# One power and one shift for both norms of a transformer block, with the second norm applied a step sooner

## The chip, the cores and the metric

One core of a Trainium2 chip (trn2). The metric is the device time of one execution in microseconds (us). The engines are TensorE (PE; its weight loads are listed as PEld), VectorE (DVE), ScalarE (ACT), GpSimd (POOL) and SyncE (SP, which here only issues DMAs). Each engine works through its own queue in order; they meet through semaphores.

## The reference

The input x has 4096 tokens of 256 channels. The output is two layers, each with its residual and a layer norm behind it:

```python
x = layernorm(x + attention(x))      # 16 heads of 16, 4 groups of keys and values, a window of 128 tokens
x = layernorm(x + channel_mix(x))    # mean and variance over the 256 channels, eps 1e-5
def channel_mix(x):                  # x_prev is x of the token before
    xr = mu_r * x + (1 - mu_r) * x_prev
    xk = mu_k * x + (1 - mu_k) * x_prev
    return sigmoid(xr @ W_r.T) * (relu(xk @ W_k.T) ** 2 @ W_v.T)
```

The layer norm is (x - m) / sqrt(v + eps), without weights. Softmax runs over the keys of the window.

## The kernel before, in words

The tokens are cut into 32 blocks of 128 (t = 0 to 31); four blocks are a superblock (s, with j = t % 4 as the place in it). The queries, keys and values of a whole superblock are projected at once and some superblocks ahead; so steps with different j carry different extra work. Everything else goes block by block in a software pipeline: `run` (L249) calls `step` of each engine for every t and, behind the last block, for five more steps that only empty the pipeline (L266). Step t holds, each for another block:

- block t + 1: the maxima of its scores (16 tiles in 6 groups: TensorE `max_scores` into PSUM banks, VectorE `tile_max`, L704, and `turn_max`, L711 to L718, whose rows SP brings to the query operand). The first groups wait for `tiles_ahead` (L696), a copy of block t + 2's queries made a step before.
- block t: its 8 score products (L969), the 8 exponentials on ScalarE (`exps`, L535) and the 8 masks on GpSimd (`mask`, L410). Two PSUM banks take turns, so score product i waits for exponential i - 2.
- block t - 1: the product with the values (L983), the copy att_t (ScalarE, L567), its turn back (TensorE, L1040), the division by the sum (VectorE `normalise`, L808 and L814), the turn of the attention (L1048) and its copy (ScalarE, L572).
- block t - 2: the output product (L1081), the first residual y1 (VectorE, L830) with its moments (L723 to L728), the power and the shift on GpSimd (`rstd`, L417 and L419), and the first norm on ScalarE (L582), a single activation with scale rstd and bias shift = -mean x rstd; then its transposition (L1032) and the copy of that (L592).
- block t - 3: the channel mix: difference to the token before (GpSimd, L470), two mixes on VectorE (L780: `mixed(u, 0)` for the r product, `mixed(u, 1)` for the k product), r product (L1059), tanh (ScalarE, L598), k product (L1070), relu and square (ScalarE).
- block t - 4: the second product (L1024), the gate (VectorE, L789), the second residual y2 (L799) with its moments, and on GpSimd its power and shift.
- block t - 5: the second norm (ScalarE, L617) and the store (SP, L342).

The order within a step is written out by hand for each engine, and the change is about these orders:

- VectorE (L834 to L868): max tiles 0 and 1, gate, max tile 2, first residual and moments, max tile 3, mixed(0), max tiles 4 and 5, `turn_max`, mixed(1), rest parts of the projection, `normalise`, `tiles_ahead`, second residual and moments, copy of vals (j = 1), a second rest part (j = 3).
- GpSimd (L473 to L502): difference, masks 0 and 1, (j = 0: a low part, L402), power and shift of block t - 2, mask 2, (j = 2: `x_plus_bo`, L396), masks 3 to 5, low parts, mask 6, power and shift of block t - 4, mask 7.
- ScalarE (L620 to L662): exponentials 0 and 1, (j = 0: a middle part), second norm of block t - 5, exponential 2, first norm, copy of att_t, (j = 3: high part 0, L517), exponential 3, tanh, (j = 0: high part 2), exponentials 4 and 5, middle parts, relu, square, exponential 6, two copies, (j = 3: high part 1), exponential 7.
- TensorE (L1085 to L1136): max scores 0 and 1, second product, max scores 2, score 0, output product, score 1, max scores 3 and 4, values 0, score 2, max scores 5, values 1, (j = 3: projection chunk 0), score 3, r product, (j = 0: chunk 2; j = 1: the turn of the values, L908), score 4, turn of att_t, score 5, k product, score 6, turn of the attention, turn of x2, (j = 3: chunk 1), score 7.

In the steps with j = 0, 1 or 2 the maxima of the next block use three PSUM banks and max scores 5 waits for max tile 2; in steps with j = 3 there are two, and it waits for max tile 3 (L937). Max scores 2 in step j = 2 goes into the bank that `val_copy` (L686) must have read.

Of the kernel before, what the change touches and what calls it, by code (L numbers as in the profile page):

```python
# [24 lines left out]
ALU = mybir.AluOpType  # L25
# [3 lines left out]
P = 128  # L29
# [25 lines left out]
def attention_channel_mix(nc, x_nat, x_feat, w_first, w_rest, out):  # L55
# [25 lines left out]
    with ExitStack() as ctx:  # L81
# [23 lines left out]
        minus_half = sb("minus_half", [P, 1])  # L105
# [25 lines left out]
        mv1 = sb("mv1", [P, 2])  # L131
        var1 = sb("var1", [P, 1])
        rstd1 = sb("rstd1", [P, 1])
        shift1 = sb("shift1", [P, 1])
# [10 lines left out]
        mv2 = sb("mv2", [P, 2])  # L145
        var2 = sb("var2", [P, 1])
        rstd2 = sb("rstd2", [P, 1])
        shift2 = sb("shift2", [P, 1])
# [50 lines left out]
        s_ln1 = sem("s_ln1")  # L199
        s_rstd1 = sem("s_rstd1")  # L200
        s_shift1 = sem("s_shift1")
# [14 lines left out]
        s_ln2 = sem("s_ln2")  # L216
        s_rstd2 = sem("s_rstd2")
        s_shift2 = sem("s_shift2")
# [30 lines left out]
        def run(eng, start, step, tail=None):  # L249
# [16 lines left out]
            for j in range(SB_BLKS, SB_BLKS + 5):  # L266
                step(NSB - 1, j, 1, project=False, coming=False, maxima=False, scores=False)
# [9 lines left out]
        def _(sp):  # L277
# [80 lines left out]
            def step(s, j, par, project, coming, maxima, scores):  # L358
# [19 lines left out]
                if behind(t, j, scores, 5):  # L378
                    store(t - 5, (j - 5) % 2)
# [10 lines left out]
        def _(pool):  # L390
# [65 lines left out]
            def step(s, j, par, project, coming, maxima, scores):  # L456
# [24 lines left out]
                if f2:  # L481
                    rstd(t - 2, var1, mv1, rstd1, shift1, s_ln1, s_rstd1, s_shift1)
# [16 lines left out]
                if f4:  # L499
                    rstd(t - 4, var2, mv2, rstd2, shift2, s_ln2, s_rstd2, s_shift2)  # L500
# [7 lines left out]
        def _(act):  # L508
# [28 lines left out]
            def start():  # L537
                act.dma_start(first[:, :], w_first).then_inc(s_first, 16)
                act.wait_ge(s_const, 1)
                nc.scalar.activation(warm[:, :], minus_half[:, :], ACT.Exp)  # L540
# [18 lines left out]
            def step(s, j, par, project, coming, maxima, scores):  # L559
                t = s * SB_BLKS + j  # L560
                ahead = project and later(s, 1)
                f1, f2, f3, f5 = (behind(t, j, scores, n) for n in (1, 2, 3, 5))
# [12 lines left out]
                def first_norm(u):  # L575

                    act.wait_ge(s_shift1, u + 1)
# [4 lines left out]
                    nc.scalar.activation(x2[:, u % 3], y1[:, :], ACT.Identity, bias=shift1[:, 0:1],  # L582
# [43 lines left out]
                if f5:  # L626
                    second_norm(t - 5)
# [554 lines left out]
```

## Time and profile before

| what | us |
|---|---|
| median of 3 runs | 453.26 |
| the 3 runs | 449.74, 453.81, 453.26 |
| span of the profiled execution | 449.1 |
| steps with j = 0, 1, 2, 3 of the superblock from 179.6 | 12.3, 11.0, 14.4, 14.0 |
| a step without projection work | 9.9 |

The span is that of the instructions of one execution. No time of its own is given for the profiled execution; the run closest to its span took 449.74, that is 0.6 more. A row of the timeline has the start, the duration, the engine and line, and in brackets how long the engine was idle before the instruction and what ended that. "xN" means N instructions merged in one row, whose duration runs from the first one's start to the last one's end. A row of windows has the stretch, its length, each engine's busy time, and the granted clock of TensorE as a share of 2.4 GHz (PEclk).

### The profile page before, as it was taken

To read this page: it belongs to the slowest core of one execution; us is meant where nothing else is said; L and a number is where in the kernel's file an instruction comes from. 1 tells how busy PE (TensorE), PEld (TensorE's weight loads), DVE (VectorE), ACT (ScalarE), POOL (GpSimd) and SP (SyncE) were. 2 spreads that over 40 slices of the span, in tenths; PEclk is the share of its full clock that TensorE was granted. 3 is DMA by queue.
4 is the path that set the end of the run, shared out by engine and by line. 5 is a ranking of instruction groups with operands and counts; after the bars stand their busy time and mean duration, and the time that the engine had idled before them with its cause. 6 is when DMAs were issued, how large, how long until landed. Compare 5 with 4: busy or idle time off the path is not lost.

```text
span 449.1 us, 8432 instructions
## 1 busy us (share of the span) xinstructions
PE 407.7 (91%) x2542; PEld 251.9 (56%) x2542; DVE 344.6 (77%) x852; ACT 272.8 (61%) x566; POOL 291.2 (65%) x466
## 2 busy tenths in 40 slices
PE   8976999997999979997999979997999979999853
PEld 3444546664556656564556665564656656665532
DVE  5765775898678976899688986799878988996551
ACT  2512567775667747764677657666577657778522
POOL 4552666776487856677487766688487767876531
PEclk9986899998999989999999989999999989999995
DMA  8484585412733175321753146421823144000000
GB/s 324 115 141 91 134 148 138 100 49 46 140 101 84 50 94 146 82 66 43 110 163 86 49 74 152 87 60 47 120 65 94 49 62 70 14 13 27 12 23 23
DMA packets 50892, 39.25 MB, mean 87 GB/s; under 512 B 33696, under 2 KB 42400, under 8 KB 50720
## 3 DMA queue, kind: packets, MB, share of 16 engines
q1 hardware_dynamic: 50416, 37.93, 38.9%
q10 hardware_dynamic: 432, 0.79, 0.6%
q8 instruction: 20, 0.33, 0.3%
q14 instruction: 24, 0.20, 0.2%
HBM read 26.38 MB, written 12.06 MB: 86 GB/s over the span
## 4 chain that ended last, share of the span: by engine, by line
PE 64%; DVE 19%; ACT 6%; issue 6%; DMA 2%; POOL 1%; SPq 1%; ACTq 0%; DVEq 0%; POOLq 0%
PE av_ps L983 11%; PE score_ps L969 9%; PE proj_ps L893 8%; PE max_ps L952 6%; PE gen L1070 6%; PE gen L1024 6%; PE gen L1081 5%; PE gen L1059 4%; DVE neg_max L704 4%; DVE q_tiles L696 3%; DVE max_parts L711 3%; PE max_ps L943 3%; ACT parts L517 2%; DVE mix L780 2%; PE av_ps L1040 2%
## 5 line engine op out<-in xcount | busy, mean ns | idle before, releaser
L410 POOL TENSOR_SCALAR_AFFINE_SELECT probs<-probs 128x512 f32<-128x512 f32 x252 | 168.2, 678 | 108.0 <-ACT probs L535 105.7
L535 ACT ACTIVATE probs<-score_ps 128x512 f32<-128x512 f32 x252 | 148.4, 598 | 86.0 <-PE score_ps L969 85.6
L969 PE MATMUL score_ps<-qs,ks 98*128 98x512 bf16 x252 | 99.8, 398 | 2.2 <-ACT probs L535 1.4
L704 DVE TENSOR_REDUCE neg_max<-max_ps 128x3 f32<-128x480 f32 x144 | 87.4, 631 | 12.3 <-PE max_ps L952 12.1
L983 PE MATMUL av_ps<-probs,vals 128*32 128x512 f32 x504 | 67.0, 605 | 0.9 <-POOL probs L410 0.8
L969 PEld LDWEIGHTS score_ps<-qs,ks 98*128 98x128 bf16 x252 | 25.0, 100 | 57.3 <-ACT probs L535 47.9
L1070 PE MATMUL gen<-mix,rest_w 128*128 128x128 f32 x256 | 38.7, 299 | 16.9 <-DVE mix L780 15.5
L952 PE MATMUL max_ps<-ks,q_tiles 96*128 96x160 bf16 x416 | 52.3, 243 | 0.0
L417 POOL TENSOR_TENSOR rstd<-var,minus_half 128x1 f32<-128x1 f32 x64 | 35.7, 558 | 21.7 <-DVE var L728 20.8
L1070 PEld LDWEIGHTS gen<-mix,rest_w 128*128 128x128 f32 x256 | 35.4, 208 | 22.7 <-DVE mix L780 17.8
L780 DVE SCALAR_TENSOR_TENSOR mix<-diff,first,x_t 128x128 f32<-128x128 f32 x128 | 43.8, 385 | 0.0
L952 PEld LDWEIGHTS max_ps<-ks,q_tiles 96*128 96x128 bf16 x416 | 37.9, 103 | 8.2 <-issue 1.9
L677 DVE SCALAR_TENSOR_TENSOR rest<-proj_ps,first,parts 128x512 f32<-128x512 f32 x19 | 14.3, 751 | 35.5 <-ACT parts L517 32.4
L893 PE MATMUL proj_ps<-x_t,first 128*128 128x512 f32 x76 | 38.3, 628 | 0.7 <-DMA first<-w_first 0.7
L943 PE MATMUL max_ps<-edge_mask,ident_b 128*128 128x192 bf16 x138 | 35.2, 255 | 3.2 <-issue 2.1
L1024 PE MATMUL gen<-rest_w,act_k 128*128 128x256 f32 x128 | 35.9, 405 | 2.1 <-ACT act_k L609 2.0
L402 POOL TENSOR_TENSOR parts<-rest,parts 128x512 bf16<-128x512 f32 x24 | 30.7, 1282 | 10.5 <-ACT parts L528 10.5
L1059 PE MATMUL gen<-rest_w,mix 128*128 128x256 f32 x128 | 34.3, 390 | 3.0 <-DVE mix L780 3.0
L1081 PE MATMUL gen<-rest_w,att_c 128*128 128x256 f32 x128 | 32.9, 379 | 0.0
L696 DVE COPY q_tiles<-qs 96x2048 bf16<-96x2048 bf16 x32 | 27.3, 853 | 5.0 <-DMA qs<-q_parts 5.0
L603 ACT ACTIVATE relu_k<-gen 128x256 f32<-128x256 f32 x32 | 12.7, 397 | 29.8 <-PE gen L1070 29.8
L582 ACT ACTIVATE x<-y,shift,rstd 128x256 f32<-128x256 f32 x32 | 19.2, 599 | 17.4 <-POOL shift L419 16.6
(86 smaller groups left out, 663.2 us busy)
## 6 DMA issues: line engine op xcount, KB each, us to landing
qs<-q_parts SPq DMA_DIRECT2D x48, 192.0 KB, 6.1
q_parts<-parts SPq DMA_DIRECT2D x48, 128.0 KB, 2.2
x_t<-x_feat SPq DMA_DIRECT2D x8, 512.0 KB, 3.7
x_in<-x_nat SPq DMA_DIRECT2D x8, 512.0 KB, 4.5
out<-out_t SPq DMA_DIRECT2D x32, 128.0 KB, 2.0
ks<-k_parts SPq DMA_DIRECT2D x42, 80.0 KB, 2.9
qs<-q_parts SPq DMA_DIRECT2D x42, 64.0 KB, 2.2
k_parts<-parts SPq DMA_DIRECT2D x8, 192.0 KB, 2.8
```

The lines of the kernel that those rows point to most:

```text
L410: nc.gpsimd.affine_select(out=v, in_=v, compare_op=ALU.is_ge if i % 2 else ALU.is_gt, fill=0.0, base=0, pattern=[[0, HPG], [sign, BLK]], c ...
L535: nc.scalar.activation(probs[:, buf, i], score_ps[i % 2][:, :], ACT.Exp, scale=SCALE).then_inc(s_exp, 1)
L704: nc.vector.tensor_reduce(neg_max[:, TPB * i:TPB * i + n], max_bank(t, j, i)[:, 0:n * TILE_KEYS].rearrange("p (n k) -> p n k", k=TILE_KEYS ...
L780: nc.vector.scalar_tensor_tensor(out=mix[:, w, c], in0=diff[:, c], scalar=small_cols[:, MU_COL + w * DC + c:MU_COL + w * DC + c + 1], in1= ...
L893: ins = nc.tensor.matmul((ps or proj_ps)[:, 0:SB], wqkv[:, c, m * P:(m + 1) * P], x_t[:, par, c], start=(c == 0), stop=(c == DC - 1))
L952: ins = nc.tensor.matmul(dst, q_tiles[:, j % 2, tile], ks[0:ROWS, par, g, k0:k0 + TILE_KEYS], start=False, stop=(k == len(tiles) - 1), ski ...
L969: nc.tensor.matmul(score_ps[i % 2][:, :].rearrange("p (h q) -> p h q", q=BLK), ks[0:ROWS + MPARTS, par, g, k0:k0 + BLK], qs[0:ROWS + MPART ...
L983: ins = nc.tensor.matmul(av_ps[g * VCOL:(g + 1) * VCOL, :], vals[:, pk, jk, g, :], probs[:, j % 2, 2 * g + half], start=(half == 0 or not ...
L1024: ins = nc.tensor.matmul(gen0[:, 0:D], act_k[:, c], w_t[:, 2, c], start=(c == 0), stop=(c == DC - 1))
L1059: ins = nc.tensor.matmul(gen0[:, 0:D], mix[:, 0, c], w_t[:, 0, c], start=(c == 0), stop=(c == DC - 1))
L1070: ins = nc.tensor.matmul(gen0[:, o * BLK:(o + 1) * BLK], w_t[:, 1, c, o * P:(o + 1) * P], mix[:, 1, c], start=(c == 0), stop=(c == DC - 1))
L1081: ins = nc.tensor.matmul(gen1[:, 0:D], att_c[:, c], wo[:, c], start=(c == 0), stop=(c == DC - 1))
```

## The change

The variables of both norms get a second column (column 0 is the first norm's, column 1 the second's). VectorE computes the second residual and its moments directly behind the first one's, no longer at the end of the step. GpSimd waits for both variances and takes one power over both columns, where the first power was; its own shifts go. VectorE computes both shifts in one instruction between max tiles 4 and 5. ScalarE applies the second norm, now of block t - 4, between the tanh and the high part or exponential 4, and SP stores it in that step. One step fewer empties the pipeline. At either end of the sequence, where only one of the two blocks exists, a single column is used.

```diff
@@ run
-            for j in range(SB_BLKS, SB_BLKS + 5):
+            for j in range(SB_BLKS, SB_BLKS + 4):
@@ SP, step
-                if behind(t, j, scores, 5):
-                    store(t - 5, (j - 5) % 2)
+                if behind(t, j, scores, 4):
+                    store(t - 4, (j - 4) % 2)
@@ GpSimd
-            def rstd(u, var, mv, out_, shift, ready, done, shifted):
-
-                pool.wait_ge(ready, u * 3 + 3)
-                nc.gpsimd.tensor_tensor(out_[:, :], var[:, :], minus_half[:, :], ALU.pow).then_inc(done, 1)
-                pool.wait_ge(done, u + 1)
-                nc.gpsimd.tensor_scalar(shift[:, :], mv[:, 0:1], out_[:, 0:1], -1.0, ALU.mult,
-                                        ALU.mult).then_inc(shifted, 1)
+            def roots(t, a, b):
+
+                for i, u in enumerate((t - 2, t - 4)):
+                    if a <= i < b:
+                        pool.wait_ge(s_var[i], u + 1)
+                nc.gpsimd.tensor_tensor(rstd[:, a:b], var[:, a:b], minus_half[:, a:b], ALU.pow).then_inc(s_rstd, 1)
...
-                if f2:
-                    rstd(t - 2, var1, mv1, rstd1, shift1, s_ln1, s_rstd1, s_shift1)
+                if f2 or f4:
+                    roots(t, 0 if f2 else 1, 2 if f4 else 1)
                 if scores and t:
                     mask(t, 2, j % 2)
...
                     mask(t, 6, j % 2)
-                if f4:
-                    rstd(t - 4, var2, mv2, rstd2, shift2, s_ln2, s_rstd2, s_shift2)
                 if scores:
                     mask(t, 7, j % 2)
@@ ScalarE
                 def second_norm(u):
 
-                    act.wait_ge(s_shift2, u + 1)
+                    act.wait_ge(s_shift, u + 3)
...
-                if f5:
-                    second_norm(t - 5)
                 if scores and t:
                     exps(t, 2, j % 2)
                 if f2:
                     first_norm(t - 2)
...
                 if f3:
                     tanh(t - 3)
+                if f4:
+                    second_norm(t - 4)
                 if ahead and j == 0:
                     high_part(s + 1, 2)
@@ VectorE
+            def shifts(t, a, b):
+
+                dve.wait_ge(s_rstd, t - 1)
+                nc.vector.scalar_tensor_tensor(out=shift[:, a:b], in0=mv[:, a:b, 0], scalar=-1.0, in1=rstd[:, a:b],
+                                               op0=ALU.mult, op1=ALU.mult).then_inc(s_shift, 1)
...
                 if f2:
                     first_residual(t - 2)
+                if f4:
+                    second_residual(t - 4)
                 if maxima:
                     tile_max(t + 1, jn, 3)
                 if f3:
                     mixed(t - 3, 0)
                 if maxima:
                     tile_max(t + 1, jn, 4)
+                if f2 or f4:
+                    shifts(t, 0 if f2 else 1, 2 if f4 else 1)
+                if maxima:
                     tile_max(t + 1, jn, 5)
                     turn_max(t + 1, j + 1)
...
                     tiles_ahead()
-                if f4:
-                    second_residual(t - 4)
                 if ahead and j == 1:
                     val_copy(s + 1, 1 - par)
```

## Rows read from the trace of the kernel before

**Rows 1.** The page, busy time of each engine (share of span, instructions).

```profile
span 449.1 us, 8432 instructions
...
PE 407.7 (91%) x2542; PEld 251.9 (56%) x2542; DVE 344.6 (77%) x852; ACT 272.8 (61%) x566; POOL 291.2 (65%) x466
```

**Rows 2.** Windows by step: j = 0, 1, 2, 3, and plain step 29.

```profile
179.60:191.90 12.30, 12.00 (x80) 7.38 (x79) 10.17 (x26) 8.99 (x20) 8.30 (x13) 1.00 0.38 81
191.90:202.90 11.00, 10.77 (x80) 7.18 (x79) 10.17 (x28) 7.56 (x17) 8.71 (x16) 1.00 0.27 70
202.90:217.30 14.40, 11.82 (x76) 7.98 (x75) 12.34 (x28) 7.62 (x17) 9.89 (x15) 0.88 0.40 72
217.30:231.30 14.00, 13.89 (x84) 8.06 (x83) 9.72 (x27) 9.73 (x21) 9.15 (x15) 1.00 0.59 137
...
390.50:400.40 9.90, 9.90 (x76) 6.76 (x75) 9.06 (x26) 7.61 (x17) 7.71 (x14) 1.00 0.06 17
```

**Rows 3.** Timeline of plain step 29: start us, duration us, engine, line.

```profile
390.23 1.03 PE L1081 MATMUL gen<-rest_w,att_c 128*128 128x256 f32 x4
...
391.60 0.42 DVE L830 TENSOR_TENSOR y<-gen,x_bo 128x256 f32<-128x256 f32 x1
...
392.79 0.15 DVE L728 TENSOR_SCALAR var<-mv 128x1 f32<-128x1 f32 x1
...
393.95 0.65 DVE L704 TENSOR_REDUCE neg_max<-max_ps 128x3 f32<-128x480 f32 x1
394.12 0.60 ACT L582 ACTIVATE x<-y,shift,rstd 128x256 f32<-128x256 f32 x1
...
395.70 0.38 ACT L598 ACTIVATE tanh_r<-gen 128x256 f32<-128x256 f32 x1
...
396.38 1.05 PE L1070 MATMUL gen<-mix,rest_w 128*128 128x128 f32 x8
...
397.80 0.84 DVE L799 SCALAR_TENSOR_TENSOR y<-gated,x 128x256 f32<-128x256 f32 x1
```

**Rows 4.** The page, costliest groups: the powers on GpSimd.

```profile
L417 POOL TENSOR_TENSOR rstd<-var,minus_half 128x1 f32<-128x1 f32 x64 | 35.7, 558 | 21.7 <-DVE var L728 20.8
```

**Rows 5.** Timeline of step 12 (j = 0).

```profile
181.92 1.16 POOL L402 TENSOR_TENSOR parts<-rest,parts 128x512 bf16<-128x512 f32 x1
...
186.50 0.69 ACT L517 ACTIVATE parts<-proj_ps,first 128x512 bf16<-128x512 f32 x1 [0.63 <-PE proj_ps L893]
...
188.65 0.44 PE L1048 MATMUL av_ps<-ident,att 128*128 128x128 f32 x2 [0.20 <-DVE att L814]
...
189.50 1.37 DVE L799 SCALAR_TENSOR_TENSOR y<-gated,x 128x256 f32<-128x256 f32 x1
```

**Rows 6.** Waits, whole trace: waiter, releaser, us in total, times, longest.

```profile
PEld proj_ps L943 <- DVE vals L686: 3.2, 6, 0.5
```

**Rows 7.** Timeline of step 14 (j = 2), and the k product of step 22.

```profile
207.13 2.36 POOL L396 TENSOR_TENSOR x_bo<-x_in,rest_w 128x1024 f32<-128x1024 f32 x1
207.24 2.28 DVE L711 CAST max_parts<-neg_max 128x16 bf16<-128x16 f32 x1
...
211.50 2.03 PE L1070 MATMUL gen<-mix,rest_w 128*128 128x128 f32 x8 [2.58 <-DVE mix L780]
...
314.71 1.16 PE L1070 MATMUL gen<-mix,rest_w 128*128 128x128 f32 x8 [2.57 <-DVE mix L780]
```

**Rows 8.** Windows: TensorE behind the hole of step 14, and the emptying pipeline.

```profile
211.50:214.90 3.40, 3.40 (x14) 2.94 (x15) 2.23 (x7) 1.30 (x4) 0.00 (x0) 0.51 0.68 124
...
430.00:436.00 6.00, 3.61 (x18) 2.50 (x18) 2.37 (x10) 2.43 (x6) 2.44 (x5) 1.00 0.03 9
```

**Rows 9.** Timeline of step 15 (j = 3): max scores 5.

```profile
220.07 0.10 PEld L943 LDWEIGHTS max_ps<-edge_mask,ident_b 128*128 128x128 bf16 x1 [0.19 <-DVE neg_max L704]
```

**Rows 10.** Timeline of the emptying pipeline, steps 33 and 34.

```profile
430.17 1.13 PE L1059 MATMUL gen<-rest_w,mix 128*128 128x256 f32 x4 [2.00 <-DVE mix L780]
...
436.76 0.42 DVE L799 SCALAR_TENSOR_TENSOR y<-gated,x 128x256 f32<-128x256 f32 x1
```

More of the change, by code:

```diff
@@ L104, in attention_channel_mix @@
         w_t = rest_w[:, D + DC * D:].rearrange("p (w c n) -> p w c n", w=3, c=DC)
-        minus_half = sb("minus_half", [P, 1])
+        minus_half = sb("minus_half", [P, 2])
         warm = sb("warm", [P, 1])
@@ L130, in attention_channel_mix @@
         stats1 = sb("stats1", [P, 6])
[L131 to L134, printed above, removed]
+        mv = sb("mv", [P, 2, 2])
+        var = sb("var", [P, 2])
+        rstd = sb("rstd", [P, 2])
+        shift = sb("shift", [P, 2])
         x2 = sb("x2", [P, 3, D])
@@ L198, in attention_channel_mix @@
         s_y1 = sem("s_y1")
-        s_ln1 = sem("s_ln1")
-        s_rstd1 = sem("s_rstd1")
-        s_shift1 = sem("s_shift1")
+        s_ln = [sem("s_ln1"), sem("s_ln2")]
+        s_var = [sem("s_var1"), sem("s_var2")]
+        s_rstd = sem("s_rstd")
+        s_shift = sem("s_shift")
         s_x2 = sem("s_x2")
@@ L539, in start @@
                 act.wait_ge(s_const, 1)
-                nc.scalar.activation(warm[:, :], minus_half[:, :], ACT.Exp)
+                nc.scalar.activation(warm[:, :], minus_half[:, 0:1], ACT.Exp)
                 act.wait_ge(s_first, 16)
@@ L561, in step @@
                 ahead = project and later(s, 1)
-                f1, f2, f3, f5 = (behind(t, j, scores, n) for n in (1, 2, 3, 5))
+                f1, f2, f3, f4 = (behind(t, j, scores, n) for n in (1, 2, 3, 4))
                 def att_t_copy():
@@ L575, in first_norm @@
                 def first_norm(u):
-                    act.wait_ge(s_shift1, u + 1)
+                    act.wait_ge(s_shift, u + 1)
                     if u >= 3:
@@ L581, in first_norm @@
                         act.wait_ge(s_y2, u - 2)
-                    nc.scalar.activation(x2[:, u % 3], y1[:, :], ACT.Identity, bias=shift1[:, 0:1],
-                                         scale=rstd1[:, 0:1]).then_inc(s_x2, 1)
+                    nc.scalar.activation(x2[:, u % 3], y1[:, :], ACT.Identity, bias=shift[:, 0:1],
+                                         scale=rstd[:, 0:1]).then_inc(s_x2, 1)
                 def x2_t_copy(u):
@@ L611, in second_norm @@
                 def second_norm(u):
-                    act.wait_ge(s_shift2, u + 1)
+                    act.wait_ge(s_shift, u + 3)
                     if u >= 2:
                         act.wait_ge(s_store[u % 2], 16 * (u // 2) + 1)
-                    nc.scalar.activation(out_t[:, u % 2], y2[:, :], ACT.Identity, bias=shift2[:, 0:1],
-                                         scale=rstd2[:, 0:1]).then_inc(s_out, 1)
+                    nc.scalar.activation(out_t[:, u % 2], y2[:, :], ACT.Identity, bias=shift[:, 1:2],
+                                         scale=rstd[:, 1:2]).then_inc(s_out, 1)
                 if scores and t:
@@ L800, in second_residual @@
                                                    in1=x2[:, u % 3], op0=ALU.mult, op1=ALU.add).then_inc(s_y2, 1)
-                    moments(u, y2, s_y2, stats2, mv2, var2, s_ln2)
+                    moments(1, u, y2, s_y2, stats2)
                 def normalise():
@@ L831, in first_residual @@
                                             ALU.add).then_inc(s_y1, 1)
-                    moments(u, y1, s_y1, stats1, mv1, var1, s_ln1)
+                    moments(0, u, y1, s_y1, stats1)
                 if maxima:
```

19 lines of the change are left out of this document (6 added, 13 removed).

## The prediction

> **What bounds the kernel now.** I read first the page's busy shares: TensorE is at 91% of a 449.1 us span and the next engine, VectorE, at 77% [rows 1]. So the question is in which steps TensorE waits. The steps of one superblock (four blocks), as windows of the trace, give 12.3, 11.0, 14.4 and 14.0 us for j = 0, 1, 2, 3, with TensorE busy 12.00, 10.77, 11.82 and 13.89 us; a plain step without projection work takes 9.9 us and TensorE is busy for all of it [rows 2]. Only j = 2 has a real hole. Everywhere else TensorE's queue is full, but only just, and that is what the change must be held against: which results come to it with how little to spare.
>
> The timeline of a plain step shows that [rows 3]. The chain of the first norm is: output product ends 391.26, first residual y (VectorE) 391.60, its variance ends 392.94, power and shift on GpSimd, norm on ScalarE at 394.12. Behind the norm, in ScalarE's queue, stand the copy of att_t, one exponential and the tanh, which ends at 396.08. TensorE's k product (L1070) waits for that tanh and starts at 396.38. **Slack: 0.30 us**, for everything that makes the norm later. The k product is followed by work of TensorE without a gap up to the next output product.
>
> **The change part by part.**
> *GpSimd.* 64 powers of 0.558 us [rows 4] become 34 (one in each of the steps 2 to 35), and 64 shifts go. Nothing of this is on the path by itself: GpSimd is 65% busy [rows 1] and its last mask of a step has cover. I cost the saving at 0 to 0.3 us a step, and take 0. But the power now waits for both variances, and the masks 2 to 7 stand behind it.
>
> *VectorE, second residual moved forward.* It is now directly behind the first residual's moments, ahead of max tile 3, mixed(0) and max tile 4. Residual to variance takes 1.34 us undisturbed (391.60 to 392.94 [rows 3]; the second residual alone 0.42 in [rows 10]), and 1.8 where the second residual takes 0.84 as in rows 3. So the second variance is 1.35 to 1.8 us later than the first.
>
> *VectorE, shift.* The instruction isn't in the trace of before; nearest are the variance's 0.15 us [rows 3] below, and, held by GpSimd, a cast of 16 columns that took 2.28 [rows 7] above. I take 0.15 where no long GpSimd instruction runs. It stands behind max tile 4. From the variance's end to that tile's end are 1.66 us (392.94 to 394.60 [rows 3]), longer than the power (0.08 + 0.56) that used to be all that lay there, with GpSimd's shift.
>
> *Plain step, sum.* The first residual can start 0.3 sooner (391.31), as VectorE's end of the step is emptier. 391.31 + 1.34 + 1.30 to 1.75 (second residual and moments) + 1.66 + 0.2 (shift) + 0.05 = 395.86 to 396.31 for the norm, against 394.12: 1.74 to 2.2 later. Less the slack of 0.30 the k product is 1.45 to 1.9 late, and all of TensorE with it. The second norm (0.60, the same form as the first), which used to sit in a hole of ScalarE ahead of exponential 2, now stands between tanh and exponential 4: 0 to 0.2. I take **1.65 us** for a plain step, bounds 1.1 and 2.1. Nothing takes it back: what left VectorE's end of the step was beside a full TensorE. Steps 28, 29, 30 and 27: 4 x 1.65 = 6.6. Step 31 (no max tiles) 0.9; steps 2 and 3, where only the shift is late, together 0.4.
>
> *j = 0.* GpSimd's low part runs 181.92 to 183.08, exactly where the second residual now comes; the one that ran beside such an instruction took 1.37 [rows 5]. So its variance ends about 184.3, tile 4 about 186.0, the norm starts about 186.2 (before 184.03), the tanh ends 188.15, and behind it now stand the second norm and only then ScalarE's high part: 188.65 against 186.50 [rows 5]. VectorE's rest part, the softmax division and TensorE's turn of the attention, which waited 0.20 for it [rows 5], follow the high part one to one: up to 2.1 us. If the second residual gets in ahead of the low part, 1.1. I take 1.9. 6 steps: 11.4.
>
> *j = 1.* Here the move also gives something: VectorE entered this step late because the second residual, 1.37 long, ended step 0, and the copy of vals stood behind it in step 1, for which TensorE waited 3.2 us in 6 times [rows 6]. The first residual starts 1.0 sooner, so the norm is late by 0.9 to 1.3 only; k product +0.75, second norm in ScalarE's queue +0.2, vals -0.3: 0.65, bounds 0 and 1.1. 6 steps: 3.9.
>
> *j = 2.* TensorE waits 2.58 us for mixed(1), since the cast L711 took 2.28 beside GpSimd's x_bo of 2.36 [rows 7]. Now power and mask 2 end 0.7 later, so x_bo runs about 207.85 to 210.2, and the shift, due at 208.4, falls into it. I let it be held to the end: norm 210.25, tanh ends 212.2, k product 212.25 against 211.50: +0.7. The rows show a cast with one input held, and the second residual with two (0.84, 1.37). The Trainium skill ("GPSIMD Engine Reference", section Key points) says that GpSimd shares its SBUF interfaces with VectorE and collides with instructions in a two-port mode or with two SBUF inputs; the new shift has two (mv and rstd), so the rule speaks for held. If it were not, the cast behind it would be held and k would come about 0.5 late, 1.2 us less in all. Bounds 0 and 1.3. 6 steps: 4.2.
>
> *j = 3.* With two banks only, max scores 5 waits for max tile 3; before, that wait was 0.19 us as the tile ran straight behind the first variance [rows 9]. Now the second residual is ahead of it: 1.35 late, and behind max scores 5 stand the value products, the projection, the r and k products. The second norm delays ScalarE's relu and high part by another 0 to 0.5. 1.6, bounds 1.3 and 2.0. 5 steps (7 to 23): 8.0.
>
> *The end.* From step 32 on, engines wait for one another in one chain. In step 32 the norm of block 30 is late and the turn of att_t with it: 1.0. In step 33 TensorE waited 2.00 us for mixed(0) [rows 10], and block 29's second residual is now ahead of that mix: 1.05. In step 34 the same with block 30: 1.35. In step 35 power, shift, norm and store of block 31 come one after another as before; that they belong to step 35 and not 36 is worth 0.1. The store's DMA was behind nothing on SP's queue that matters. Sum 3.4, bounds 2.4 and 4.0.
>
> *The clock.* In 5 of the 6 steps with j = 2 the granted clock fell to 0.51 (1.2 instead of 2.4 GHz) behind the 2.58 us hole; 3.40 us of TensorE work then did what 1.7 do at full clock [rows 8]. It is a near thing: behind 2.57 us of waiting the k product of another superblock took 1.16 instead of 2.03 us [rows 7]. After the change the hole is cut in two (about 2.2, then the turn of att_t, then 0.3), so I let 2 of the 5 falls go: -3.4, bounds -8.5 and 0.
>
> **Sum.** 6.6 + 0.9 + 0.4 + 11.4 + 3.9 + 4.2 + 8.0 + 3.4 - 3.4 = +35.4, so a span of 484.5 from 449.1. The runs shown have 449.74, 453.81 and 453.26; which was profiled is not given. The median is 4.2 above the span, and I add the sum to it: 453.3 + 35.4 = **489 us**. All parts at their lower bounds, with all five falls gone: 4.4 + 0.6 + 0 + 6.6 + 0 + 0 + 6.5 + 2.4 - 8.5 = +12; all at the upper: 8.4 + 1.2 + 0.8 + 12.6 + 6.6 + 7.8 + 10 + 4 = +51. They won't all lie on one side; its own range is 478 to 501.
>
> **The rivals.**
> *Half of it is hidden (chance 0.17).* The second residual slips in ahead of the low part, the shift ahead of x_bo, ScalarE finds holes for the second norm, and all clock falls go. For it: VectorE's end of each step is 1.8 us emptier. Against: the first norm's wait is in every step. Near the lower bounds, some +16: 469.
> *The clock falls in more places (0.11).* Every step now has a hole of about 1 us on TensorE. One fall more in each step with j = 0 and j = 3: 11 x 1.7 = 19, so 508. Against: from 430 to 436 TensorE was busy for 3.61 of 6.00 us, with a hole of 2.00, and the clock stayed at 1.00 [rows 8, 10].
> *Not slower (0.05).* The mechanism: what limits the steps is VectorE's tail (second residual, then vals and the first max tiles), and the norm's lateness disappears in ScalarE's queue. Then step 1 gets back 1.05 and vals 0.3, 8 us in six superblocks: 445. It decides from the point where the norm is less than 0.30 us late; the rows make it 1.7.
> *The merge is not worth what it says (inside the first).* GpSimd's saved 0.9 us a step doesn't appear in the time at all; what does is only where the second residual stands.
>
> **How the numbers follow.** Forecast 0.67, the others 0.17, 0.11, 0.05. The range for 8 in 10 runs from the centre of the half-hidden case to short of the clock case: 469 to 504. A measurement of this kernel tells about 1% from no change. Faster by over 1%: 0.04; within 1%: 0.02; slower: 0.94.
>
> **What would show it.** Right: in a plain step the norm (L582) starts 1.7 to 2.2 us later behind the output product, tanh ends just ahead of the k product, step length about 11.5; in j = 3 TensorE waits about 1.4 for max tile 3; ScalarE's largest new wait is for VectorE's shift; a second residual of over 1 us in j = 0; a shift of 1 us or more in j = 2 alone. Wrong: plain steps still at 9.9 us, or a shift that starts right behind the power, or TensorE's share still over 90%.

## The result, and the profile after

The changed kernel takes 497.23 us (median of 4 runs, 495.6 to 503.29); the kernel before, with one more run beside it, 451.8. The ratio is **1.097** (95% interval 1.089 to 1.105): slower, as forecast (489 us, range 469 to 504). Executions of one kernel differ in how often TensorE's clock fell, and the profiled ones of three experiments below (the shift sooner, the second residual behind the first mix, and the shift behind max tile 5 in the steps with j = 0) lie above the medians of their runs, so their step lengths may hold more falls than a median run does. The profiled execution has a span of 495.0 us, 45.9 more than before; the forecast's sum was +35.4.

The page of the kernel after, with its largest waits (waiter, releaser, us in total, times, longest):

```profile
span 495.0 us, 8400 instructions
...
PE 423.2 (85%) x2540; PEld 254.8 (51%) x2542; DVE 340.2 (69%) x886; ACT 268.3 (54%) x566; POOL 259.4 (52%) x372
...
L573 ACT ACTIVATE x<-y,shift,rstd 128x256 f32<-128x256 f32 x32 | 19.2, 599 | 83.3 <-DVE shift L724 83.3
...
L413 POOL TENSOR_TENSOR rstd<-var,minus_half 128x2 f32<-128x2 f32 (+1 forms) x34 | 23.2, 683 | 56.8 <-DVE var L719 56.8
```

```profile
ACT x L573 <- DVE shift L724: 83.3, 31, 5.3
...
PEld gen L1059 <- DVE mix L777: 33.1, 26, 3.7
...
PEld av_ps L1040 <- ACT att_t L558: 26.3, 19, 3.1
```

GpSimd's work fell from 291.2 to 259.4 us and nothing of it came back as time: every engine is busy for a smaller share of the span, since each waits for another. TensorE is down from 91% [rows 1] to 85%. ScalarE waits 83.3 us for the new shift. TensorE waits for two things for which it hardly waited before: its weight loads wait 33.1 us for the mix ahead of the r product (6.2 before) and 26.3 for the copy of att_t behind the norm (2.5 before).

Windows by step, for the same steps as [rows 2] (12 to 15, j = 0 to 3, and the plain step 29):

```profile
190.90:205.10 14.20, 12.34 (x79) 7.29 (x79) 11.47 (x30) 9.02 (x19) 8.76 (x13) 1.00 0.33 69
205.10:216.50 11.40, 10.97 (x80) 7.00 (x79) 9.22 (x28) 7.31 (x16) 5.80 (x9) 1.00 0.27 72
216.50:231.30 14.80, 11.79 (x76) 8.00 (x75) 11.13 (x28) 7.42 (x16) 9.50 (x12) 0.88 0.33 56
231.30:246.80 15.50, 13.99 (x84) 8.07 (x83) 9.52 (x29) 9.72 (x20) 8.01 (x13) 1.00 0.69 136
...
424.90:436.30 11.40, 10.59 (x75) 6.63 (x75) 8.89 (x27) 7.31 (x16) 6.38 (x11) 1.00 0.05 14
```

Step lengths against the forecast (I take each step's start from ScalarE's first exponential in the two timelines and add up the steps of one kind):

| steps | forecast, us | measured, us |
|---|---|---|
| j = 0, six | +11.4 | +11.9 |
| j = 1, six | +3.9 | +3.0 |
| j = 2, six, clock falls included | 4.2 - 3.4 = +0.8 | +7.8 |
| j = 3, five | +8.0 | +7.5 |
| plain 27 to 30 | +6.6 | +6.3 |
| 2 and 3 | +0.4 | 0 |
| 31 and the emptying of the pipeline | +4.3 | +8.1 |
| ahead of step 2 | 0 | +1.4 |

Of the terms of the sum, five hold to within a microsecond. Two failed by more: j = 2 by 7.0 us and the end by 3.8, and TensorE's clock has a part in both. Ahead of step 2, where the changed code does not run, the profiles of all the kernels here lie between 51.1 and 55.0 us, so +1.4 says nothing of the change.

The timeline of the plain step 29, which answers to [rows 3]:

```profile
424.74 1.03 PE L1081 MATMUL gen<-rest_w,att_c 128*128 128x256 f32 x4
...
425.80 0.42 DVE L827 TENSOR_TENSOR y<-gen,x_bo 128x256 f32<-128x256 f32 x1 [0.39 <-PE gen L1081]
...
427.12 0.53 DVE L796 SCALAR_TENSOR_TENSOR y<-gated,x 128x256 f32<-128x256 f32 x1
...
428.44 0.15 DVE L719 TENSOR_SCALAR var<-mv 128x1 f32<-128x1 f32 x1
...
428.74 0.70 POOL L413 TENSOR_TENSOR rstd<-var,minus_half 128x2 f32<-128x2 f32 x1 [1.36 <-DVE var L719]
...
429.73 1.13 PE L1059 MATMUL gen<-rest_w,mix 128*128 128x256 f32 x4 [0.42 <-DVE mix L777]
430.16 0.15 DVE L724 SCALAR_TENSOR_TENSOR shift<-mv,rstd 128x2 f32<-128x2 f32 x1
...
430.35 0.60 ACT L573 ACTIVATE x<-y,shift,rstd 128x256 f32<-128x256 f32 x1 [1.82 <-DVE shift L724]
...
431.47 0.66 PE L1040 MATMUL av_ps<-ident,att_t 128*128 128x128 f32 x4 [0.39 <-ACT att_t L558]
...
431.81 0.38 ACT L589 ACTIVATE tanh_r<-gen 128x256 f32<-128x256 f32 x1
...
432.33 1.13 PE L1070 MATMUL gen<-mix,rest_w 128*128 128x128 f32 x8
```

From the end of the output product (425.77) to the norm are 4.58 us, against 2.86 before (394.12 - 391.26): 1.72 later, the forecast had 1.74 to 2.2. The tanh ends at 432.19 and the k product starts at 432.33, right behind it, 1.44 later than before counted from the output product. Between power's end (429.44) and shift (430.16) lie 0.72 us in which the shift waits for nothing but its turn behind max tile 4. TensorE stands twice, for the mix and for att_t.

The norm's path was not the only tight one. In the kernel before, VectorE's mixed(1), for which the k product waits as well, ended at 396.00, that is 0.38 us ahead of the k product (396.38), hardly more than the 0.30 that the tanh had:

```profile
395.43 0.57 DVE L780 SCALAR_TENSOR_TENSOR mix<-diff,first,x_t 128x128 f32<-128x128 f32 x2
```

In the kernel after, mixed(1) ends at 431.71 and the tanh at 432.19, so the norm's path is the later one, by 0.48.

In step 12 (j = 0) the second residual runs beside GpSimd's low part and takes 1.37, and the high part, now behind the second norm, starts 199.80 - 190.92 = 8.9 us into the step instead of 7.0. In step 15 (j = 3) max scores 5 waits for max tile 3, 1.69 instead of 0.19 [rows 9]:

```profile
193.34 1.16 POOL L396 TENSOR_TENSOR parts<-rest,parts 128x512 bf16<-128x512 f32 x1
193.41 1.37 DVE L796 SCALAR_TENSOR_TENSOR y<-gated,x 128x256 f32<-128x256 f32 x1
...
235.74 0.10 PEld L943 LDWEIGHTS max_ps<-edge_mask,ident_b 128*128 128x128 bf16 x1 [1.69 <-DVE neg_max L695]
```

Step 14 (j = 2), which answers to [rows 7]:

```profile
221.80 2.34 POOL L390 TENSOR_TENSOR x_bo<-x_in,rest_w 128x1024 f32<-128x1024 f32 x1
221.82 2.34 DVE L724 SCALAR_TENSOR_TENSOR shift<-mv,rstd 128x2 f32<-128x2 f32 x1
224.20 0.60 ACT L573 ACTIVATE x<-y,shift,rstd 128x256 f32<-128x256 f32 x1 [4.02 <-DVE shift L724]
...
225.32 1.11 PE L1040 MATMUL av_ps<-ident,att_t 128*128 128x128 f32 x4 [2.58 <-ACT att_t L558]
...
226.66 1.82 PE L1070 MATMUL gen<-mix,rest_w 128*128 128x128 f32 x8
```

A shift over two columns, 0.15 us elsewhere, takes 2.34 beside x_bo: it starts 0.02 behind x_bo and ends 0.02 behind it. It was so in all six steps of this kind (2.33 or 2.34), and so was TensorE's wait for att_t, 2.57 or 2.58.

### The profile page after: what moved, and what is told of

Read it like the earlier page. It is cut to its first block, busy times and chain, and to the rows that moved or that the text cites. A ratio compares the mean times of both kernels' runs of the same rounds, so it can differ in the third digit from the quotient of the medians.

```text
span 495.0 us, 8400 instructions
## 1 busy us (share of the span) xinstructions
PE 423.2 (85%) x2540; PEld 254.8 (51%) x2542; DVE 340.2 (69%) x886; ACT 268.3 (54%) x566; POOL 259.4 (52%) x372
## 4 chain that ended last, share of the span: by engine, by line
PE 40%; DVE 32%; ACT 14%; issue 9%; DMA 2%; POOL 1%; SPq 1%; ACTq 0%; DVEq 0%; POOLq 0%
DVE neg_max L695 7%; DVE stats L714 5%; PE gen L1024 5%; PE gen L1070 5%; PE score_ps L969 5%; PE gen L1081 5%; DVE y L796 4%; ACT probs L526 4%; PE proj_ps L893 3%; PE max_ps L952 3%; DVE shift L724 3%; ACT parts L508 3%; PE av_ps L1040 3%; DVE y L827 3%; DVE mix L777 2%
## 5 line engine op out<-in xcount | busy, mean ns | idle before, releaser
L526 ACT ACTIVATE probs<-score_ps 128x512 f32<-128x512 f32 x252 | 146.8, 599 | 95.3 <-PE score_ps L969 95.3
L573 ACT ACTIVATE x<-y,shift,rstd 128x256 f32<-128x256 f32 x32 | 19.2, 599 | 83.3 <-DVE shift L724 83.3
L1059 PE MATMUL gen<-rest_w,mix 128*128 128x256 f32 x128 | 37.3, 416 | 24.2 <-DVE mix L777 24.2
L413 POOL TENSOR_TENSOR rstd<-var,minus_half 128x2 f32<-128x2 f32 (+1 forms) x34 | 23.2, 683 | 56.8 <-DVE var L719 56.8
L943 PE MATMUL max_ps<-edge_mask,ident_b 128*128 128x192 bf16 x138 | 34.7, 251 | 12.3 <-DVE neg_max L695 8.8
L1070 PE MATMUL gen<-mix,rest_w 128*128 128x128 f32 x256 | 42.1, 317 | 1.1 <-ACT tanh_r L589 1.1
L1070 PEld LDWEIGHTS gen<-mix,rest_w 128*128 128x128 f32 x256 | 38.6, 225 | 7.8 <-issue 7.0
L1059 PEld LDWEIGHTS gen<-rest_w,mix 128*128 128x128 f32 x128 | 23.2, 197 | 36.9 <-DVE mix L777 33.1
L777 DVE SCALAR_TENSOR_TENSOR mix<-diff,first,x_t 128x128 f32<-128x128 f32 x128 | 38.3, 340 | 0.2 <-issue 0.2
L1040 PE MATMUL av_ps<-ident,att_t 128*128 128x128 f32 x128 | 22.1, 299 | 17.9 <-ACT att_t L558 17.9
L396 POOL TENSOR_TENSOR parts<-rest,parts 128x512 bf16<-128x512 f32 x24 | 30.7, 1285 | 10.2 <-ACT parts L519 10.2
```

The source lines that it names most:

```text
L526: nc.scalar.activation(probs[:, buf, i], score_ps[i % 2][:, :], ACT.Exp, scale=SCALE).then_inc(s_exp, 1)
L777: nc.vector.scalar_tensor_tensor(out=mix[:, w, c], in0=diff[:, c], scalar=small_cols[:, MU_COL + w * DC + c:MU_COL + w * DC + c + 1], in1= ...
L1059: ins = nc.tensor.matmul(gen0[:, 0:D], mix[:, 0, c], w_t[:, 0, c], start=(c == 0), stop=(c == DC - 1))
L1070: ins = nc.tensor.matmul(gen0[:, o * BLK:(o + 1) * BLK], w_t[:, 1, c, o * P:(o + 1) * P], mix[:, 1, c], start=(c == 0), stop=(c == DC - 1))
```

## The experiments

The theories. **Theory 1**: what counts is VectorE's order; the second residual and two max tiles stand ahead of the shift, and the second residual ahead of max tile 3 and mixed(0). **Theory 2**: what counts is that GpSimd's power waits for both variances. **Theory 3**: the shift on VectorE and the second norm's place on ScalarE cost as much as the move. All ratios below are to the kernel before, run on the same chip.

### One power or two

```diff
-                if f2 or f4:
-                    roots(t, 0 if f2 else 1, 2 if f4 else 1)
+                if f2:
+                    roots(t, 0, 1)
                 if scores and t:
                     mask(t, 2, j % 2)
+                if f4:
+                    roots(t, 1, 2)
```

> The changed kernel, but GpSimd takes the first norm's power right behind the first variance (one column), and the second's behind mask 2; VectorE's order and the one shift stay. Theory 1 (VectorE's order holds the norm: second residual, max tiles 3 and 4 stand ahead of the shift): the shift starts where it did, so 494 to 500 us, at most 3 us gained by earlier masks. Theory 2 (GpSimd's joint wait for both variances holds it): the first power is 1.4 us sooner in each step, so about 30 us gained, near 467.

486.62 us, ratio 1.069 (1.062 to 1.076), between the two expectations, so neither number came true. The step lengths say where: the plain steps are still 11.5 us, j = 0 still 14.2, j = 3 still 15.5, j = 1 still 11.5. Only j = 2 changed, in its windows beside a plain step:

```profile
214.40:227.70 13.30, 10.62 (x76) 6.67 (x75) 10.79 (x27) 7.30 (x17) 9.44 (x13) 1.00 0.28 54
414.40:425.90 11.50, 10.67 (x76) 6.71 (x75) 8.99 (x27) 7.34 (x17) 6.89 (x12) 1.00 0.05 14
```

```profile
222.74 0.66 PE L1042 MATMUL av_ps<-ident,att_t 128*128 128x128 f32 x4 [2.23 <-ACT att_t L560]
```

So theory 2 falls for the steps of every kind but that one: the power was 1.4 us sooner and the plain step didn't move. In j = 2 the shift is held for 1.99 instead of 2.34 us, and TensorE's wait for att_t is 2.23 or 2.24 instead of 2.58. In four of the six such steps there was no fall of the clock and they took 13.3 us, where the changed kernel, with a fall in each, took 14.8 to 16.3.

### The shift sooner

```diff
                 if f3:
                     mixed(t - 3, 0)
+                if f2 or f4:
+                    shifts(t, 0 if f2 else 1, 2 if f4 else 1)
                 if maxima:
                     tile_max(t + 1, jn, 4)
-                if f2 or f4:
-                    shifts(t, 0 if f2 else 1, 2 if f4 else 1)
-                if maxima:
                     tile_max(t + 1, jn, 5)
```

> The changed kernel with the one shift directly behind mixed(0), ahead of max tile 4. Theory 1: the norm is 0.5 to 0.65 us sooner in each of some 28 steps, and in j = 2 the shift gets in ahead of x_bo, so 12 to 20 us gained: 477 to 485. Theory 2: the power is the limit and it ends just ahead of this place; 0 to 4 us gained: 493 to 497.

Ratio 1.088 (1.076 to 1.100), median 500.74: both numbers are missed, and by the ratio this kernel can't be told from the changed one. The line of the shift in this kernel (minimum, median, maximum in ns):

```profile
L724 DVE SCALAR_TENSOR_TENSOR shift<-mv,rstd x34: 147/587/593, 57.3 to 499.6; 128x2 f32<-128x2 f32 x30, 128x1 f32<-128x1 f32 x4
```

The shift no longer meets x_bo, but now it meets mask 2, which GpSimd starts the moment the power is done, and takes 0.59 instead of 0.15. The norm came only 0.13 us sooner in a plain step (4.42 against 4.55 us behind y1). In j = 2 it came 2.3 us sooner (4.42 against 6.74) and the step still took 15.4: there the cast behind the shift is held instead, and the k product waits 2.40 us for its other operand, mixed(1). And in four of the steps with j = 0 the clock fell, and they took 15.8 to 16.4 instead of 14.2.

### The second residual moved, alone

```diff
                 if f2:
                     first_residual(t - 2)
+                if f4:
+                    second_residual(t - 4)
...
                     tiles_ahead()
-                if f4:
-                    second_residual(t - 4)
```

(in the kernel before, with its own powers and shifts)

> The kernel before, with one edit: VectorE's second residual and moments stand behind the first ones; powers, shifts and second norm as before. Theory 1: mixed(0) is 1.35 to 1.8 us late but the norm isn't; plain steps +0.5 (the tanh behind the r product), j = 3 +1.4 (max tile 3), j = 0 +0.5, pipeline's end +2.4: 15 to 22 us slower than before, 467 to 474. Theory 2: the move costs nothing by itself, 450 to 455.

487.51 us, ratio **1.070** (1.064 to 1.077): the right sign, but 32 us where 15 to 22 were expected. The move alone makes 32 of the 45 us. A plain step:

```profile
417.90:429.00 11.10, 10.47 (x76) 6.73 (x75) 8.96 (x26) 7.70 (x17) 7.71 (x15) 1.00 0.05 15
```

and in its timeline:

```profile
421.40 0.60 ACT L582 ACTIVATE x<-y,shift,rstd 128x256 f32<-128x256 f32 x1
...
422.68 1.13 PE L1059 MATMUL gen<-rest_w,mix 128*128 128x256 f32 x4 [0.44 <-DVE mix L780]
...
423.87 0.60 PE L1040 MATMUL av_ps<-ident,att_t 128*128 128x128 f32 x4
...
424.88 1.16 PE L1070 MATMUL gen<-mix,rest_w 128*128 128x128 f32 x8 [0.19 <-DVE mix L780]
```

Here the norm is on time (2.7 us behind the output product), and yet the step is 1.2 longer: the r product waits for mixed(0), and then the k product for mixed(1), which stands behind everything else on VectorE. So in the plain step **two** paths lead from the moved residual to the k product, by the norm and by the mixes. The mixes' path costs 1.2 alone, and the norm's on top of it brings the step to 11.4; what the norm's would cost alone was not run. My expectation had counted only the r product's lateness.

The same holds for j = 0, and there it changes the account. In step 12 of this kernel, which starts at 188.16 and takes 14.1 us:

```profile
194.09 1.13 PE L1059 MATMUL gen<-rest_w,mix 128*128 128x256 f32 x4 [1.55 <-DVE mix L780]
...
195.06 1.88 PE L893 MATMUL proj_ps<-x_t,first 128*128 128x512 f32 x4
...
196.97 0.69 ACT L517 ACTIVATE parts<-proj_ps,first 128x512 bf16<-128x512 f32 x1 [1.33 <-PE proj_ps L893]
```

The norm is on time (4.66 us into the step, 4.52 before) and the second norm is out of the way, and yet the high part starts 8.8 us into the step, as in the changed kernel (8.9; before 7.0). It waits for projection chunk 2, which stands behind the r product on TensorE, and the r product waits 1.55 us for mixed(0). The move alone makes 10.9 of the 11.9 us of the steps with j = 0, and all of the loss with j = 3 (7.9, the changed kernel 7.5).

### Idle work for TensorE while the pipeline empties

```diff
+                if not scores and j > SB_BLKS:
+                    keep_running(max_ps[0], 4)
```

(behind the r product, the k product and the turn of x2)

> The changed kernel with 4 idle matmuls (512 columns, bf16, 0.22 us each at full clock) behind the r product, the k product and the turn of x2 in steps 33 to 35. If the end's 8 us instead of the 3.4 forecast come from the clock, which fell at 470.6 and stayed at 1.2 GHz, the clock now stays up longer and 3 to 6 us go: 491 to 494. If they come from waits alone, the time is the same or up to 2 us longer.

494.72 us, ratio 1.088 (1.079 to 1.096); the interval overlaps that of the changed kernel, so the total tells little. The windows do. Of the changed kernel, the end:

```profile
470.60:495.00 24.40, 12.82 (x34) 8.57 (x34) 6.27 (x24) 4.80 (x11) 2.50 (x4) 0.50 0.05 16
```

and of this one:

```profile
476.60:492.60 16.00, 10.65 (x53) 6.23 (x51) 4.62 (x16) 3.12 (x8) 1.79 (x3) 1.00 0.05 17
```

The clock came back to 1.00. The clock fell inside the wait for block 30's mixed(0), as in the changed kernel, and was back at 1.00 after 6.8 us. From the first mix of block 31 to its gate are 6.2 us here and 8.4 in the changed kernel. That is 2.2 us for the clock in that stretch. From step 31 to the end only 1.4 are gained, so 0.8 was lost again elsewhere; there the k product of block 30, behind idle matmuls at half clock, started 0.9 later behind the r product than in the changed kernel.

### One power for t - 2 and t - 5

The second norm's power can be shared with the first without moving the residual, if it takes the block whose variance was finished at the end of the step before:

```diff
-                for i, u in enumerate((t - 2, t - 4)):
+                for i, u in enumerate((t - 2, t - 5)):
...
                     tiles_ahead()
+                if f4:
+                    second_residual(t - 4)
```

(and second norm, shift, store and the emptying steps for t - 5 in place of t - 4), once with the shift behind max tile 4 and once directly behind mixed(0).

> One power and one shift as in the changed kernel, but for the first norm of block t-2 and the second of t-5, so VectorE's second residual can stay at the end of the step as before; shift behind max tile 4, second norm behind the tanh. Theory 1 (where the second residual stands makes most of the loss): 3.3 us from y1 to norm instead of 2.5, so 0.2 to 0.5 us a step: 0.5 to 2.5% slower than before. Theory 3 (the shift on VectorE and the second norm in ScalarE's queue cost as much as the move): 4% slower or more.

> As the one with t-5, and the shift directly behind mixed(0). Theory 1: mask 2 on GpSimd holds the shift (0.59 instead of 0.15 as in the run with the early shift), norm 2.9 to 3.1 us behind y1, inside or just beyond the slack of 0.3: within 1% of before. Theory 3: 3% slower or more.

Ratios **1.006** (1.003 to 1.010) and **0.996** (0.992 to 1.000). Both hold for theory 1, and theory 3 falls: with the second residual where it was, one power, one shift on VectorE and the second norm behind the tanh stay within 1% of the time before. With the late shift a plain step took 10.4 us, the norm 3.54 behind y1 (before: 2.52); with the early one 9.9 and 2.54. In single steps they are not free. In the profile of the second version only the clock gains, with two falls in the steps with j = 2 instead of five, while its steps with j = 0 took 13.1 instead of 12.3; the first version had three such falls.

### x_plus_bo in four pieces, before and after

```diff
-                if ahead and j == 2:
-                    x_plus_bo(s + 1, 1 - par)
...
                     mask(t, 6, j % 2)
+                if ahead:
+                    x_plus_bo_piece(s + 1, 1 - par, j)
```

(a piece adds one block of 256 columns and waits for that block's old x_bo to be read; s_xbo counts blocks)

> The kernel before with x_plus_bo (2.36 us in the steps with j = 2) cut into four pieces of one block each (about 0.6 us), one in each step, behind mask 6. If the hole in j = 2 comes from VectorE being held by that one GpSimd instruction, these steps fall from 14.4 (12.8 without a clock fall) to 10 to 10.5 us, no clock falls remain there, and the piece costs 0 to 0.2 a step: 4 to 6% faster than before. If it is the work itself and not its place, no change.

> The changed kernel with the same four pieces. The shift is nowhere over 1 us, the steps with j = 2 become like the plain ones, 11.4 to 11.8 us instead of 14.8 to 16.3, no clock falls there: 20 to 25 us less than the changed kernel, so 4 to 5.5% slower than before. If j = 2 is long for another reason (the second residual's place), under 8 us less.

Before with the pieces: 430.27 us, ratio **0.943** (0.937 to 0.950). After with the pieces: 474.05, ratio 1.042 (1.035 to 1.048). The steps with j = 2 in the first:

```profile
193.40:203.90 10.50, 10.10 (x76) 6.70 (x75) 9.65 (x28) 7.58 (x17) 8.39 (x15) 1.00 0.41 75
```

10.5 instead of 14.4 [rows 2], in all six of them, and no fall of the clock between 46.4 and 408.2 us. In the second they took 11.4 in all six, as long as a plain step. So the one GpSimd instruction of 2.36 us, where it stood, had cost each kernel about 25 us. The edit makes it shorter and moves it at once; which of the two counts was not tried apart. The change's own loss, with this out of the way, is about 10% (1.042 / 0.943), much as with it.

### The second residual behind the first mix

```diff
-                if f4:
-                    second_residual(t - 4)
                 if maxima:
                     tile_max(t + 1, jn, 3)
                 if f3:
                     mixed(t - 3, 0)
+                if f4:
+                    second_residual(t - 4)
```

> The changed kernel with VectorE's second residual and moments behind max tile 3 and mixed(0) instead of ahead of them; shift still behind max tile 4, so the norm is as late as in the changed kernel (4.5 us behind y1), while the r product and max scores 5 get theirs on time. If the norm's path alone holds a plain step, it stays at 11.4; if it needs both, it falls to 10.5 or less. Steps with j = 3 lose their wait for max tile 3 and 1 us or more; the end of the pipeline, where mixed(0) was held twice, gets 2 to 3 us back. 1.06 to 1.085 times before.

510.86 us, ratio **1.118** (1.110 to 1.127): worse than the changed kernel, outside the expectation of 1.06 to 1.085. Three steps in a row without projection work, and the wait in one:

```profile
416.30:430.00 13.70, 12.02 (x75) 7.88 (x74) 9.21 (x28) 7.41 (x16) 6.09 (x11) 0.88 0.43 60
430.00:443.70 13.70, 11.96 (x75) 7.87 (x75) 9.16 (x27) 7.41 (x16) 6.18 (x11) 0.88 0.04 10
443.70:457.40 13.70, 11.97 (x75) 7.87 (x75) 9.17 (x27) 7.41 (x16) 6.18 (x11) 0.88 0.04 11
```

```profile
450.61 0.57 DVE L724 SCALAR_TENSOR_TENSOR shift<-mv,rstd 128x2 f32<-128x2 f32 x1 [0.31 <-POOL rstd L413]
...
452.34 0.66 PE L1040 MATMUL av_ps<-ident,att_t 128*128 128x128 f32 x4 [1.73 <-ACT att_t L558]
```

The r product is on time here, as expected. But the shift now also waits for the power and is held by mask 2, so the norm is 5.20 us behind y1 instead of 4.55, and TensorE's two short holes of the changed kernel (0.42 and 0.39) have become one of 1.73. The granted clock fell once in each plain step, which then took 13.7 instead of 11.4. Of what was expected of j = 3 half came (15.0 instead of 15.5, where 1 us or more was expected): max tile 3 is on time, but high part 0 stands behind the late norm on ScalarE and starts 7.05 us into step 15 instead of the 6.07 of the kernel before. The end of the pipeline gave 1.3 us back (46.2 instead of 47.5 from step 31 on), where 2 to 3 were expected.

### The pieces and the shared power together

> One power and one early shift for t-2 and t-5, the second residual at the end of the step, and x_plus_bo in four pieces: the two edits that were not slower than before, together. If they add, 0.935 to 0.95 times before; if the merge is worth something once GpSimd is fuller, below 0.935; if the shift or the longer second norm's place collides with the pieces, above 0.95.

438.68 us, ratio 0.961 (0.953 to 0.969), above the 0.95 of the expectation: they don't add. Once the pieces are in, there are no falls in j = 2 left for the shared power to save, and its cost in j = 0 stays, 13.2 us:

```profile
174.00:187.20 13.20, 12.31 (x80) 7.38 (x79) 10.70 (x27) 9.05 (x20) 8.78 (x12) 1.00 0.53 139
```

```profile
178.27 0.57 DVE L726 SCALAR_TENSOR_TENSOR shift<-mv,rstd 128x2 f32<-128x2 f32 x1 [0.33 <-POOL rstd L415]
...
179.79 1.95 PE L894 MATMUL proj_ps<-x_t,first 128*128 128x512 f32 x4 [0.59 <-DVE neg_max L697]
```

The early shift delays max tile 5, and projection chunk 2 goes into the bank that this tile reads. To test that, the shift was put behind tile 5 in these steps alone:

```diff
-                if f2 or f5:
+                if (f2 or f5) and not (ahead and j == 0):
                     shifts(t, 0 if f2 else 1, 2 if f5 else 1)
...
                     tile_max(t + 1, jn, 5)
+                if (f2 or f5) and ahead and j == 0:
+                    shifts(t, 0 if f2 else 1, 2 if f5 else 1)
```

> As the last (t-2 with t-5, early shift, four pieces), but in the steps with j = 0 the shift stands behind max tile 5 instead of ahead of tile 4. There the early shift waited 0.33 for the power and was held to 0.57, which made tile 5 late and with it projection chunk 2 (TensorE waited 0.59 for that tile); those steps took 13.2 us instead of 12.3. If that is the whole of what the merge cost on top of the pieces, j = 0 falls to 12.3 to 12.6 and the time to within 1% of the kernel before with the pieces alone. If the second norm ahead of the high part costs it, j = 0 stays at 13 or more.

> The kernel before with x_plus_bo in four pieces once more, as the partner of the other on the same chip: 0.937 to 0.95 times before, 427 to 433 us.

The step with j = 0 fell to 12.5 us as expected:

```profile
174.60:187.10 12.50, 12.05 (x80) 7.44 (x79) 10.13 (x27) 8.93 (x20) 8.67 (x12) 1.00 0.56 147
```

435.08 us (ratio 0.954, 0.923 to 0.985) beside 431.0 for the pieces alone (0.950, 0.933 to 0.967). The two can't be told apart in the total, and the shared power doesn't gain anything even now. The lowest ratio found is that of the kernel before with x_plus_bo in pieces: two rounds gave 0.943 (0.937 to 0.950) and 0.950.

## Why the prediction was right, and where it was not

*The slack of 0.30 us and the norm's chain.* Right. The norm was 1.72 us later behind the output product, the k product 1.44, the plain steps 1.5 to 1.8 longer.

*That nothing takes it back.* Right. VectorE's emptier end of the step (idle 1.19 us ahead of max tile 0 in the plain step) was beside a full TensorE.

*j = 1 and 3.* Right within 1 us for each group of steps: max scores 5 waits 1.4 to 1.7 us for max tile 3, and a step with j = 1 is 0.5 longer, where 0.65 was forecast.

*j = 0.* The sum is right (11.9 for 11.4), and so is the second residual held by the low part (1.37). But the number does not rest on the path that was given for it, by the norm, the tanh and the second norm. With the norm on time the run with the residual moved alone has 10.9 of it, by mixed(0), the r product and projection chunk 2, and in the changed kernel both paths reach the high part within 0.1 us of one another. The forecast did not have the second one, so that the sum came out is in part luck.

*The shift held by x_bo.* Right: 2.33 or 2.34 us in each of the six steps. The rule cited from the Trainium skill ("GPSIMD Engine Reference", Key points), that an instruction of VectorE with two SBUF inputs collides with GpSimd, agrees with it, and with the 0.59 beside mask 2 in the run with the early shift.

*"I let 2 of the 5 falls go."* **This term failed.** There were falls in all six steps with j = 2, and two of them lasted twice as long (6.8 us instead of 3.4). The forecast cut the hole to about 2.2 us, for which its working gives no sum; it measured 2.58, the same as before. The norm came 7.60 us into the step where 7.44 was reckoned (both from ScalarE's first exponential, 216.60 and 202.81), and the power of two columns, 0.70 instead of the 0.56 used, is most of that difference. Instead of -3.4 + 4.2 = 0.8 these steps cost 7.8. A step without a fall would have taken about 13.6 (an estimate: the 13.3 of the run with two powers and the 0.35 by which its hole is shorter), 0.8 more than the one such step before that had none (12.8, step 22). So the 0.7 for the held shift was about right, and by the same estimate the falls cost 2.7 more than before where 3.4 less was forecast.

Nor does the size of the hole tell the number of falls. In the one profile that each kernel has, a hole of 2.57 to 2.64 us went with five falls in six such steps before and six in six after, but one of 2.58 with two in six where t - 2 and t - 5 share the power and the shift is early; one of 2.40 with three in six (the same with the late shift) and with six in six (the shift sooner in the changed kernel); one of 2.23 with two in six (two powers). What decides beside the hole stays open.

*The end.* The mixes' and the norm's lateness were forecast at 3.4 and step 31 at 0.9; together they took 8.1. In step 33 TensorE's wait for mixed(0) grew from 2.00 [rows 10] to 3.32, by 1.32 where 1.05 was reckoned:

```profile
471.75 2.08 PE L1059 MATMUL gen<-rest_w,mix 128*128 128x256 f32 x4 [3.32 <-DVE mix L777]
472.21 0.60 ACT L573 ACTIVATE x<-y,shift,rstd 128x256 f32<-128x256 f32 x1 [5.30 <-DVE shift L724]
```

But the clock fell inside that wait, 24.4 us ahead of the end instead of 12.2, and the r product took 2.08 instead of 1.13. The run with idle matmuls showed 2.2 us of the 3.8 that were missing, behind block 31's first mix alone. How the remaining 1.6 us divide between the clock in step 33 and longer waits was not tried apart.

*The path that was missed.* The forecast reasoned by the norm alone. The run with the residual moved alone shows a second path, by the mixes, which makes a plain step 1.2 us longer by itself. In the changed kernel mixed(1) lies 0.48 us in the shadow of the norm's path, so the sum for the plain step came out right. The expectation for the run with the residual moved alone left it out, and was too low by that and by the steps with j = 0 (0.5 us each expected, 1.8 measured).

*The share of the merge.* The last rival said that GpSimd's saving wouldn't appear and the place of the second residual would be all. The runs show it: 1.070 for the move alone, 0.996 and 1.006 for the merge alone. 1.097 for both together is more than their product (1.066 to 1.076). Of the 10.2 us between the profile of the changed kernel and that of the move alone, 3.8 lie in the steps with j = 2, 2.2 at the end, 1.4 with j = 1, 1.2 in the plain steps and 1.0 with j = 0. In the changed kernel the shift stands behind the second residual, and in j = 2 it meets x_bo; that this makes the whole excess is argued and not shown.

*The other rivals.* None came. Beyond its slack nothing of the first norm's lateness was hidden. The clock stayed up in the steps with j = 0 and 3 of the changed kernel, though TensorE waits 1.55 us for mixed(0) in step 12 and 1.4 to 1.7 for max tile 3; in the run with the early shift it fell in four steps with j = 0.

## What to carry to other kernels

To share one instruction between two pieces of work, share it with a piece that is already finished (t - 5 here, 0.996 and 1.006), not with one whose work must be moved ahead of the urgent one's to meet it (1.097). Before moving work forward in an engine's queue, count everything behind the new place and the slack of each consumer (0.30 us for the norm and 0.38 for mixed(1) here), not the room at the old place. A long GpSimd instruction beside VectorE's small ones is the first thing to look for in a step with a hole: cut up and placed behind mask 6, 2.36 us gave 5 to 6% of the whole.

## What the runs showed of the hardware that was not expected

- A power over two columns takes 0.70 us on GpSimd and over one 0.55, so sharing it saves 0.40 of 1.10, less than half.
- A two-column instruction of VectorE with two SBUF inputs that starts behind a GpSimd instruction is held until that ends: 0.15 us alone, 0.57 to 0.59 beside a mask, 1.99 and 2.34 beside x_bo, each time ending 0.01 or 0.02 behind the GpSimd instruction. The second residual, 0.42 alone, took 0.53 beside a mask and 1.37 beside a low part, and ended 0.27 or 0.28 behind it. So what it costs is above all what is left of the GpSimd instruction when it starts.
- From step 4 on TensorE's clock fell behind holes of 1.55 to 2.64 us, and not behind each. Holes of 0.42 and 0.39 in a plain step left it at 1.00; with one of 1.73 in each plain step it fell once per step, 13.7 instead of 11.4 us. In the changed kernel holes of 1.55 us in step 12 and 2.07 in step 16 left it at 1.00, and with x_bo in pieces one of 1.55 in step 8 was followed by a fall. In j = 2 a hole 0.35 us shorter went with four falls fewer of six, but holes of the same 2.58 us went with two falls in one kernel and six in another.
